# Second cross attention: every piece of a hand-written stream at a new position

## What is computed

```
q = rope(x @ Wq)            # 512 tokens, 32 heads of 16
k, v = split(ctx @ Wkv)     # 512 context tokens; k = rope(k)
w = softmax(q @ k.T / 4)
x = layernorm(x + (w @ v) @ Wout + bout)
```

## Time and profile before

| what | us |
|---|---|
| median of 3 runs | 2783.61 (2780.51 to 2786.38) |
| the profiled execution | 2809.74 |
| its span | 2807.9 |
| second cross attention in it, first turned tile to last output matmul | 1953.6 to 2610.3 |
| from the first to the last score piece | 1990.7 to 2568.3 |

### The profile page before, as it was taken

One profiled execution on the slowest core, in us unless ns is written; L12 is line 12 of the kernel. 1 busy time (PEld: TensorE's weight loads), 2 busy tenths in 40 slices (PEclk: granted clock), 3 DMA queues, 4 the chain that ended last, 5 costly groups with the idle time before them and its releaser, 6 DMA issues. The chain is left out here.

```text
span 2807.9 us, 39805 instructions
## 1 busy us (share of the span) xinstructions
PE 2615.2 (93%) x12494; PEld 1690.4 (60%) x12494; DVE 1796.8 (64%) x3475; ACT 1370.2 (49%) x2910; POOL 302.9 (11%) x402
## 2 busy tenths in 40 slices
PE   8999998888799987999999999999899999998898
PEld 6667664444588873676776777776555545443343
DVE  6767765634443326755756756755677777785687
ACT  5455453321133322455455455554577667676453
POOL 1111014003401114000000000000201110100000
PEclk9999999989899998999999999999999999999999
DMA  7654538522587763333223223221000000002323
GB/s 270 160 140 144 148 76 268 202 75 98 167 266 236 243 188 126 138 106 101 82 106 99 83 105 108 80 91 56 6 10 2 9 2 6 2 2 54 68 68 83
DMA packets 176492, 299.88 MB, mean 107 GB/s; under 512 B 73712, under 2 KB 96256, under 8 KB 175520
## 3 DMA queue, kind: packets, MB, share of 16 engines
q1 hardware_dynamic: 159424, 244.72, 27.7%
q0 software_dynamic: 16864, 52.65, 7.1%
HBM read 221.55 MB, written 64.77 MB: 102 GB/s over the span
## 5 line engine op out<-in xcount | busy, mean ns | idle before, releaser
L2667 DVE TENSOR_REDUCE x_neg_max<-bank 128x1 f32<-128x512 f32 x512 | 327.0, 683 | 96.7 <-PE bank L2511 96.2
L2618 ACT ACTIVATE x_weights<-bank 128x512 f32<-128x512 f32 x512 | 279.1, 599 | 130.2 <-PE bank L2522 125.2
L2024 ACT ACTIVATE a_probs<-bank,a_neg_max 128x128 f32<-128x128 f32 (+3 forms) x256 | 136.1, 532 | 211.6 <-DVE a_neg_max L2120 207.0
L1924 PE MATMUL bank<-a_x_high,a_weights 128*128 128x512 f32 x640 | 223.4, 413 | 16.8 <-issue 7.5
L123 PEld LDWEIGHTS bank<-all_ident,a_probs 128*128 128x128 f32 x1200 | 151.4, 140 | 84.3 <-issue 46.2
L123 PE MATMUL bank<-all_ident,a_probs 128*128 128x128 f32 x1200 | 193.4, 273 | 2.2 <-ACT a_probs_t L2016 2.2
L2016 ACT COPY a_probs_t<-bank 128x128 f32<-128x128 f32 (+3 forms) x256 | 107.5, 420 | 144.3 <-PE bank L123 143.8
L1959 PE MATMUL bank<-a_k_cols,a_q_cols 128*128 128x128 f32 (+3 forms) x512 | 176.7, 434 | 0.5 <-DVE a_q_cols L2069 0.3
L1988 PE MATMUL bank<-a_wo,a_att_high 128*128 128x512 f32 x512 | 162.2, 398 | 3.8 <-DVE a_q_cols L2069 2.9
L1645 DVE TENSOR_TENSOR moe_acc<-bank,moe_acc 128x512 f32 x79 | 54.6, 692 | 173.5 <-PE bank L1309 173.3
L1298 PE MATMUL bank<-moe_gh_cols,moe_item 128*128 128x256 f32 x632 | 152.5, 385 | 5.0 <-DMA moe_item<-moe_items 4.6
(11 more groups left out here) (411 smaller groups left out, 5361.8 us busy)
## 6 DMA issues: line engine op xcount, KB each, us to landing
a_weights<-split_qkv SPq DMA_DIRECT2D x80, 512.0 KB, 3.6
moe_item<-moe_items SPq DMA_DIRECT2D x79, 257.0 KB, 4.1
moe_item<-moe_items SPq DMA_DIRECT2D x79, 256.0 KB, 3.6
a_pieces<-split_qkv SPq DMA_DIRECT2D x36, 512.0 KB, 3.7
a_wo<-split_out SPq DMA_DIRECT2D x8, 2048.0 KB, 8.1
a_wo<-split_out SPq DMA_DIRECT2D x16, 1024.0 KB, 10.3
split_qkv<-x_qkv_parts SPq DMA_DIRECT2D x12, 1024.0 KB, 5.0
moe_items<-in_L_ffn_e_w POOLq DMA_DIRECT2D x40, 256.0 KB, 6.4
```

Source lines behind the costliest of these rows:

```text
L1924: last = pe.matmul(mm[g % 2], weight[:, k, :], x[:, k, :], start=n == 0, stop=n == 3 * KD - 1)
L2618: act.activation(weights[:, chunk % 2, k, :], weight_banks[slot % 2], ACT.Exp).then_inc(s.weight.free, 1)
L2667: dve.tensor_reduce(neg_max[:, g % 2, j, h:h + 1], score_banks[slot % 3], AX.X, ALU.max, negate=True) \
```

## The change

Only positions change. The list holds the same 1524 pieces, with the same instructions, semaphores and buffers. `scores`, `weights` and `values` get an offset of their own for each of the 8 steps (4 value pieces) of a group, and all entries of the two tables are new. Some of the shape of the diff:

```
-    WEIGHTS_AT, VALUES_AT, COPY_AT, BACK_AT, TURN_AT, LATE_CONTEXT_AT = -1.929, 1.112, 1.113, 2.282, 0.434, 2.8
+    SCORES_AT = (0.356, 0.178, -0.272, 0.55, 0.441, -0.143, 0.322, 0.85)
+    WEIGHTS_AT = (-1.798, -2.105, -1.477, -1.423, -1.584, -1.763, -2.193, -1.423)
+    VALUES_AT = (2.083, 0.509, 1.962, 0.707)
+    COPY_AT, BACK_AT, TURN_AT, LATE_CONTEXT_AT = 2.523, 8.655, 0.672, 2.8
     NEXT_UNIT = (
...
-            (7.74, 'rope_mul', 'q', 1), (8.71, 'pad', 'q', 1, 0), (9.23, 'rope_swap', 'q', 1),
...
+            (4.0, 'fill', 'q', 1, 2), (4.9, 'fill', 'q', 1, 3), (5.632, 'rope_mul', 'q', 1),
+            (8.346, 'high', 'q', 0), (8.79, 'rope_swap', 'q', 1), (9.193, 'rope_add', 'q', 1),
+            (9.288, 'low', 'q', 0), (9.547, 'pad', 'q', 1, 0), (9.57, 'c', 1), (9.931, 'high', 'q', 1),
...
     OUTPUT = (
-        (16.5, 'feats', 3), (17.78, 'feats', 2), (18.54, 'feats', 0), (24.09, 'feats', 1), (32.45, 'out', 0, 0),
...
-        (57.95, 'out', 3, 1), (58.1, 'out', 3, 2), (59.05, 'out', 3, 3), (59.94, 'ln_add', 3), (63.55, 'ln_var'),
-        (66.17, 'ln_norm', 3), (67.87, 'ln_norm', 1), (68.08, 'ln_norm', 0), (76.05, 'ln_norm', 2),
+        (24.773, 'feats', 0), (25.322, 'feats', 2), (26.936, 'feats', 3), (30.612, 'feats', 1),
...
+        (57.241, 'out', 3, 1), (58.537, 'out', 3, 2), (61.527, 'out', 3, 3), (61.745, 'ln_add', 3),
+        (62.245, 'ln_var'), (63.245, 'ln_norm', 3), (63.245, 'ln_norm', 1), (63.245, 'ln_norm', 0),
+        (63.245, 'ln_norm', 2),
     )
...
-            place(u * STEPS + n, ("scores", u, n))
+            place(u * STEPS + n + SCORES_AT[n % GS], ("scores", u, n))
...
-            place(u * STEPS + n + LAG + WEIGHTS_AT, ("weights", u, n))
+            place(u * STEPS + n + LAG + WEIGHTS_AT[n % GS], ("weights", u, n))
...
-            place(u * STEPS + 2 * n + LAG + VALUES_AT, ("values", u, n))
+            place(u * STEPS + 2 * n + LAG + VALUES_AT[n % NT], ("values", u, n))
...
-            place(end - 1 + 0.04, ("shift_split", u, g))
+            place(end - 1 + 0.04 + max(0, *[SCORES_AT[n] - (GS - 1 - n) for n in range(GS)]), ("shift_split", u, g))
```

More of the change, by code:

```diff
@@ L2224, in cross_attention_1 @@
     OUTPUT = (
-        (16.5, 'feats', 3), (17.78, 'feats', 2), (18.54, 'feats', 0), (24.09, 'feats', 1), (32.45, 'out', 0, 0),
-        (34.86, 'out', 0, 1), (36.61, 'out', 0, 2), (38.41, 'out', 0, 3), (38.88, 'ln_add', 0), (46.69, 'out', 1, 0),
-        (46.81, 'out', 1, 1), (48.09, 'out', 1, 2), (48.92, 'out', 1, 3), (49.13, 'ln_add', 1), (50.15, 'out', 2, 0),
-        (50.92, 'out', 2, 1), (54.87, 'out', 2, 2), (56.42, 'out', 3, 0), (56.54, 'out', 2, 3), (57.92, 'ln_add', 2),
-        (57.95, 'out', 3, 1), (58.1, 'out', 3, 2), (59.05, 'out', 3, 3), (59.94, 'ln_add', 3), (63.55, 'ln_var'),
-        (66.17, 'ln_norm', 3), (67.87, 'ln_norm', 1), (68.08, 'ln_norm', 0), (76.05, 'ln_norm', 2),
+        (24.773, 'feats', 0), (25.322, 'feats', 2), (26.936, 'feats', 3), (30.612, 'feats', 1),
+        (37.512, 'out', 0, 0), (39.136, 'out', 0, 1), (39.931, 'out', 0, 2), (40.048, 'out', 0, 3),
+        (40.321, 'ln_add', 0), (49.362, 'out', 1, 0), (50.363, 'out', 1, 1), (50.705, 'out', 1, 2),
+        (51.017, 'out', 1, 3), (51.039, 'ln_add', 1), (52.016, 'out', 2, 0), (53.345, 'out', 2, 1),
+        (53.918, 'out', 2, 2), (55.297, 'out', 2, 3), (56.67, 'ln_add', 2), (57.076, 'out', 3, 0),
+        (57.241, 'out', 3, 1), (58.537, 'out', 3, 2), (61.527, 'out', 3, 3), (61.745, 'ln_add', 3),
+        (62.245, 'ln_var'), (63.245, 'ln_norm', 3), (63.245, 'ln_norm', 1), (63.245, 'ln_norm', 0),
+        (63.245, 'ln_norm', 2),
     )
```

## The result

The changed kernel takes **2798.61 us** (median of 8 runs, 2791.39 to 2806.29) against 2783.19 for the kernel before beside it (8 runs). The ratio is 1.0056, with a 95% interval of 1.0044 to 1.0068: slower by some 15.6 us, where 4.4 us less were forecast. The profiled execution took 2806.29 us, span 2804.5.

A forecast was written before the change was run, and what follows sets the result against it. TensorE was taken as the bound, with 58.8 us of waits to win. Terms -2.3 - 13 - 6 + 15.5 + 3.4 - 2 = -4.4 us, so 2783.6 becomes 2779; forecast's own range 2768 to 2790, full range 2752 to 2800.

The forecast's parts named there:

- the block: Four normalisations in one gap at the ends of units 3, 5 and 7: waits +15.5 us, lower clock +3.4.
- ordinary waits: TensorE's thinly spread waits in 29 plain groups: mean gain 0.45 us a group, -13 us, bounds 0 and -35.
- the tail: Behind unit 7's last scores: TensorE waits 5.7 us at the turn, ACT is the bound there; the end gives -1 us.
- group (1,16), shift collision: Bias pieces on POOL slowed DVE's splits in the shift of group (1,8); collision gone, -6 us, bounds -6 and 0.
- 29 other groups, with least values: Groups not named singly: ordinary waits -13 us, and -2.3 us from TensorE's fewer changes of kind.
- prologue: At the start, three pads behind the first score piece, first fill of q ahead of two turned tiles: -1 us.
- Rival C: Bias pieces on the shared port delay `rope_add` in three units instead: -6 becomes -2, time 2783; chance 0.07.
- hand-walks: Groups (2,8), (2,16), (3,8) followed in the new order: 16.6 plus 0.9 of waits, 17.4 plus 0.2, 15.8 plus 1.8.
- Waits ahead of L2531 should all but vanish: At the turn of the shift, 8.3 us waiting for ACT's bank in 20 cases; now a value piece covers it.
- B: Rival, slower: pauses at the ends of units 3 and 5 bring 10 to 15 us of clock cost; time 2798; chance 0.23.
- A: Rival: ordinary waits go nearly all, groups keep 0.1 to 0.2 us each; -13 becomes about -33, time 2759; chance 0.22.
- D: Rival: the order hardly matters, a wait removed in one gap returns in the next; time 2784; chance 0.08.

The follow-up runs named there:

- e2: The kernel before with only its four normalisations moved into one gap, between score pieces 30 and 31 of units 3, 5 and 7; ratio 1.0103.
- e1: The changed kernel with the four normalisations of each batch apart again, at the kernel before's position numbers; ratio 1.0007, measured again 1.0004.
- e3: The changed kernel with only the normalisations of batch 2, which lie in the tail, back at their old positions; ratio 1.0014.
- e4: The changed kernel plus five fp32 matmuls with unused results ahead of the last shift turn, so TensorE works through that pause; ratio 1.0038.
- e6: e5 with the output pieces, ln_add and ln_var of batch 2 at the places of the kernel before; ratio 0.9976 to the kernel before.
- e9: e5 with two of the four normalisations back in the gap at the border, behind the last scores of units 3 and 5; ratio 0.9999.
- e5: e3 with the normalisations of batches 0 and 1 put one each into gaps of units 4 and 6 with DVE slack; ratio 0.9976.
- e10: e5 with ACT's copy of a unit's last group moved behind weight piece 2 of the next unit, seven swaps; ratio 0.9941 to the kernel before.
- e8: e5 with the stream pieces that prepare the next unit (table NEXT_UNIT) at the kernel before's places, offsets still new; ratio 1.0144.
- e7: e6 with all offsets of the last unit (scores, weights, values, copy, back, shift) as in the kernel before; ratio 0.9987.

## Why the prediction was wrong, point by point

The mechanism that spoke against the change, the block, was seen, and sized rightly at two of its three places. Two other terms failed, and they make up 17 of the 20 us between forecast and result: unit 7's share of the ordinary waits (off by 9.7 us) and the tail (off by 7.3). What they have in common is the clock. The forecast priced time at half clock behind the two blocks only, and put it at nothing in unit 7 and in the tail.

| term | forecast | measured |
|---|---|---|
| group (1,16), shift collision | -6 | -6.2 |
| blocks at units 4 and 6, waits and clock | +13.2 | +13.9 |
| 29 other groups, with least values | -15.3 | -2.7 |
| of these the 4 of unit 7 | -2.1 | +7.6 |
| prologue | -1 | -1.3 |
| tail, block and end | +4.7 | +12.0 |
| sum | -4.4 | +15.7 |

- **Collision on POOL: the size came in part by luck.** (1,16) took 16.3 us instead of 22.4. But e2, with the old order and the same collision, took 18.7 there: 3.7 us of the gain are the 10.2 us at half clock that only the profile of before has. The new order took 14.8 us where no half clock fell into the group (e1, e3, e4, e6 and e9), so at full clock the gain is 3.9. The bias piece at 2072.12 no longer meets the splits. `low` of k does, but a value piece covers it, and the turn waits only 0.16 us:

```profile
2070.88 1.28 POOL L2763 TENSOR_TENSOR x_split<-x_rot,x_split 128x512 fp32r<-128x512 f32 x1 [5.96 <-ACT x_split L2610]
2070.94 1.26 DVE L2684 TENSOR_TENSOR x_shift<-x_neg_max,x_shift 128x16 fp32r<-128x16 f32 x1
...
2072.12 0.68 DVE L2709 TENSOR_TENSOR x_rot<-bank,all_up 128x512 f32<-128x512 f32 x1
2072.12 1.28 POOL L2769 TENSOR_TENSOR all_x_tok<-all_x_tok,x_bout_row 128x512 f32<-128x512 f32 x1
```

The second split of 128x16 took 1.26 us, as long as POOL's instruction beside it, where the forecast had 0.18 us for each. The `rope_mul` beside the bias piece has one operand in a bank and ran undisturbed, 0.68 us. Rival C's victim, `rope_add`, did not appear: all 28 of them from the first score piece on took 0.69 us.
- **Blocks at units 3 and 5: right.** "The distance from the start of s31 to that of the next score piece should be close to 6 for its second half": it was 6.27 (2250.75 to 2257.02 in unit 3) and 5.95 us, the waits 4.47 and 4.15. With them came 3.4 and 6.8 us at half clock, where 3.4 each were forecast.
- **Ordinary waits: the hand-walks were right, the extrapolation to unit 7 was not.** Groups (2,8), (2,16) and (3,8) took 17.8, 17.8 and 17.6 us where 17.5, 17.6 and 17.6 were foreseen. The 25 plain groups of units 0 to 6 gained 10.3 us of the 13.2 that this step gave them. But -0.45 a group was carried over to unit 7, where none was walked. There the order of the outputs differs and no fills cover the waits. Its four groups changed by +3.2, +0.9, +3.7 and -0.2 us, with 10.2 us at half clock where the kernel before had none. The clock's part can be estimated from kernels with the same order of unit 7 up to its last pieces: 65.5 us with 3.4 us at half clock (e1, e3), 66.7 and 67.0 with 6.8 (e5, e9), 68.6 with 10.2 (the changed kernel and e4), thus 0.35 to 0.45 us for each. That makes some 4 of the 7.6 us. Least values make 1.1. What makes the remaining 2 to 3 us, and what brings the half clock there, stays open; no pause like that of the blocks stands in unit 7.
- **The wait for the shift.** "Waits ahead of L2531 should all but vanish": besides the tail's 4.83, L2539 waits 1.1 us in its 31 other turns (the 5.9 of the group's row less 4.83). The row of the kernel before has 4.4 for all 32, and e10's has 0.6. The direction is right, the size was not: the row below gives 2.8 us to ACT's bank where the forecast names 8.3.

```profile
L2531 PE MATMUL bank<-all_ident,x_shift 128*8 128x128 f32 x128 | 19.2, 271 | 4.4 <-ACT x_weights L2618 2.8 <-DVE x_shift L2676 1.1
```

- **The tail: the clock was put at nothing.** The forecast priced the third pause at 5.7 and its clock at nothing, as "in the tail of unit 7 ACT is the bound". The pause was 4.8. The clock was the larger part. Seven kernels have the same order in the tail and no pause in it: it takes 41.2 us with 3.4 us at half clock (e3), 42.1 to 42.4 with 6.8 (e5, e8, e10), 46.6 and 47.0 with 20.5 (e6, e9) and 48.6 with 23.9 (e1), some 0.3 to 0.35 us for each microsecond. For the changed kernel, whose 27.3 us lie in part within the pause, that makes some 8 of the 12.0 us, beside 4.8 of pause and 1 gained at the end, as forecast. e3 (11.8 us back from 4.8 us of pause) and e4 (3.0 us back with the wait left in) show it independently. The step failed in logic: "ACT is the bound" was read at full clock, where ACT's and TensorE's loads stand close (e3's rows). At half clock TensorE is busy 12.79 of 13.70 us and ACT 7.18 (e1's row), so TensorE is the bound again.
- **Rivals.** B gave 2798 and the time is 2798.6, but its mechanism was the stretches behind units 3 and 5, over 8 us each. They were 3.4 and 6.8. That the number met is luck; its clock loss was real but lay in unit 7 and the tail. A is refuted as written: the groups did not come out 0.1 to 0.2 us from their least values. e10 reaches some of it, with the copy that the forecast had named as what "holds it back", at 0.5 to 1 us a unit; measured 0.8 (5.9 us over seven). D is refuted as well: order alone moved the ratio from 0.9941 to 1.0486.

Taken together, main part and tail have 44.3 us more at half clock than before. At 0.3 to 0.45 us each this is, as an estimate, 13 to 20 us, about as much as the whole loss; the forecast had 3.4 us for it.

The Trainium skill (TensorE: Matmul & The Clock Gate, section What's actually happening) makes the lower level the default and the higher one a thing that activity has to keep. The traces agree for all three pauses. They don't show why e1's tail stays at the lower level for 13.7 us with TensorE busy 12.8 of them.

## What to carry to other kernels

Work of an engine that is not the bound may still not be piled up in one gap: four DVE steps of 1.22 us cost 7 us a place with the clock behind them, one each in gaps with an estimated 1.2 us or more of slack cost 0 to 0.9. "Another engine is the bound here" is a statement at one clock; behind a pause price TensorE's work at half rate and see who is the bound then. A gain read from one profile can hold clock that another run of the same order doesn't have (22.4 and 18.7 us for one group). And positions written by hand are one fit: judged one part at a time, new offsets with the old stream were 1.4% slower than the kernel before, old offsets of weights and values alone with the new stream 4.9%, while moving a single ACT copy by one place in seven units gave 0.3%.

## What the runs showed of the hardware

- Half-speed stretches repeated for the same kernel. Two kernels profiled twice had them at the same pieces, 20.5 and 13.7 us long. But they don't belong to the local order alone. e1 and e3 have the same tail order, and 23.9 against 3.4 us at half clock in it; they differ last in unit 6. The kernel before and e2 have the same order up to unit 3, and 10.2 against 0 us behind the same collision in unit 1. What decides this stays open, and how other executions of one kernel differ (e9's two kinds, 9 us apart) was not profiled.
- How long it lasts doesn't follow from the pause. With waits of 4.47 and 4.15 us came 3.4 and 6.8 us at half clock, with one of 4.83 came 20.5, with one of 1.55 came 3.4, and with one of 1.72, in e7, 17.1. With the wait of 1.08 us in the earlier trace rows came 10.2, and with the same wait in e2 none.
- In the tail TensorE shows 17.7 of 20.4 us busy at half clock. Its busy share alone (4.4 of 5 us in e3) would not tell that stretch from one at the full clock; the mean of a value piece (1.91 against 1.05 us) and the granted clock do.
- A DVE instruction with both operands in SBUF (the split of 128x16, 0.18 us elsewhere) took 1.26 us beside a POOL instruction of 1.28; one with an operand in a bank ran at its usual 0.68 us beside POOL.
